# Q projected once and doubled by VectorE shuffles, h copied by VectorE, z one maximum later

## The reference

```python
h = tok(x)                                   # (16, 221, 128): three patch projections, bias, position
z = layernorm(h); q, k, v = split(z @ w_qkv.T)
a = softmax(q @ k.T / sqrt(16)) @ v          # per head
h = h + a @ w_agg.T + b_agg
z = layernorm(h)                             # first 1024 tokens, two experts each
h = h + sum_k weight_k * (gelu(z @ w1[e_k]) @ w2[e_k])
```

## Time and profile before

| | |
|---|---|
| median of 3 runs | 271.49 us (271.13 to 271.51) |
| profiled execution | 271.6 us, its span 270.0 us |
| granted TensorE clock over the span | 0.991 |
| TensorE busy | 255.9 us (95%) |
| VectorE busy | 211.9 us (78%) |
| ScalarE busy | 143.3 us (53%) |
| GpSimd busy | 114.9 us (43%) |

### The profile page before, as it was taken

How to read it: one execution, slowest core, us unless ns; L and a number is a source line. 1 busy time by engine, 2 the same in 40 slices (tenths; PEclk the granted TensorE clock), 3 DMA queues, 4 the chain that set the end, 5 groups by cost and what they waited for, 6 DMA issues and landing times.

```text
span 270.0 us, 7288 instructions
## 1 busy us (share of the span) xinstructions
PE 255.9 (95%) x2925; PEld 222.1 (82%) x2925; DVE 211.9 (78%) x453; ACT 143.3 (53%) x223; POOL 114.9 (43%) x178
## 2 busy tenths in 40 slices
PE   8999989999899999999998999999999999998991
PEld 8899977879697979797977979888888888887771
DVE  2976489879989878898968869696969697877684
ACT  4770332725251615252447676777768585869240
POOL 4000031203348474747573546656474838353200
PEclk9999999999999999999999999999999999999996
DMA  6999200089100000000021102011111111000252
GB/s 210 417 389 438 125 1 2 0 277 301 48 24 14 23 14 26 13 27 9 28 51 30 47 12 54 30 40 39 40 39 43 40 30 39 13 26 31 84 143 85
DMA packets 15623, 22.29 MB, mean 83 GB/s; under 512 B 2415, under 2 KB 10327, under 8 KB 15559
## 3 DMA queue, kind: packets, MB, share of 16 engines
q1 hardware_dynamic: 13447, 18.67, 21.1%
q0 software_dynamic: 1760, 2.60, 3.1%
q10 hardware_dynamic: 384, 0.57, 0.7%
HBM read 17.43 MB, written 5.95 MB: 87 GB/s over the span
## 4 chain that ended last, share of the span: by engine, by line
PE 70%; DVE 15%; ACT 6%; issue 4%; DMA 2%; POOL 1%; SPq 0%; DVEq 0%; POOLq 0%; ACTq 0%
PE e_ps L1153 11%; PE s_ps L1239 11%; PE s_ps L1153 8%; PE e_ps L1435 7%; PE m_ps L1353 7%; PE m_ps L1420 5%; PE m_ps L1224 5%; DVE nmax L903 4%; ACT L668 3%; PE e_ps L1420 3%; PE m_ps L1214 3%; DMA x_raw<-x 2%; PE m_ps L1383 2%; DVE x_lo L790 2%; PE m_ps L1203 1%
## 5 line engine op out<-in xcount | busy, mean ns | idle before, releaser
L903 DVE TENSOR_REDUCE nmax<-s_ps 128x4 fp32r<-128x884 f32 (+1 forms) x60 | 61.8, 1070 | 15.5 <-PE s_ps L1239 14.8
L620 ACT ACTIVATE probs<-s_ps 128x888 f32<-128x888 f32 (+1 forms) x60 | 51.4, 910 | 23.2 <-PE s_ps L1239 23.2
L517 POOL DMA_INDIRECT y_rows<-y_sb,idx_u x23 | 23.1, 1003 | 28.4 <-PE s_ps L1239 25.6
L462 POOL TENSOR_TENSOR var_eps<-mv,eps_t 128x2 f32<-128x2 f32 x16 | 5.6, 350 | 68.8 <-DVE mv L862 68.8
L495 POOL DMA_INDIRECT z_slots<-z,slot_u x20 | 23.4, 1170 | 15.8 <-PE s_ps L1239 11.4
L1353 PE MATMUL m_ps<-probs,v_aug 128*32 128x221 f32 (+1 forms) x480 | 25.8, 353 | 0.0
L1435 PE MATMUL e_ps<-w_now,hidT 128*128 128x128 f32 x184 | 23.2, 275 | 0.0
L1435 PEld LDWEIGHTS e_ps<-w_now,hidT 128*128 128x128 f32 x184 | 22.4, 192 | 0.1
L604 ACT COPY zT<-m_ps 128x221 f32<-128x221 f32 x16 | 5.5, 344 | 30.0 <-PE m_ps L1204 30.0
L1239 PE MATMUL s_ps<-k_a,q_hi 32*128 32x222 f32 (+1 forms) x252 | 19.1, 309 | 2.0 <-DVE nmax L903 1.1
L1153 PE MATMUL e_ps<-x_hi,w_hi 128*128 128x252 f32 (+2 forms) x128 | 20.7, 294 | 0.1
(11 more groups left out here) (169 smaller groups left out, 613.9 us busy)
## 6 DMA issues: line engine op xcount, KB each, us to landing
w_raw<-wt SPq DMA_DIRECT2D x6, 512.0 KB, 10.1
x_raw<-x SPq DMA_DIRECT2D x6, 512.0 KB, 10.5
w_sb<-w SPq DMA_DIRECT2D x1, 2048.0 KB, 9.9
z_slots<-z SPq DMA_DIRECT2D x1, 1518.0 KB, 13.8
zs<-z_slots SPq DMA_DIRECT2D x7, 198.0 KB, 2.6
x_raw<-x SPq DMA_DIRECT2D x4, 256.0 KB, 5.5
out<-h SPq DMA_DIRECT2D x11, 64.0 KB
c_sb<-consts SPq DMA_DIRECT2D x1, 599.5 KB, 13.2
```

What stands on the lines that cost most here:

```text
L517: g.indirect_dma_start(y_dram, bass.IndirectOffsetOnAxis(ap=idx_u[:, at:at + 1], axis=0), y_sb[:, n % 2, i, :], None).then_inc(y_out[n % 2 ...
L620: s.activation(probs[0:n, blk, 2 * f:2 * f + 2].rearrange("p t u n -> p t (u n)"), s_ps[0:n, 2 * f:2 * f + 2, 0:2 * NE], ACT.Exp, scale=DH ...
L903: v.tensor_reduce(nmax[0:n, blk, 2 * f:2 * f + 2, DH:DH + 2], src, AX_X, ALU.max, negate=True).then_inc(max_ready, 1)
```

## The change

For batches from DOUBLED = 8 on, q is projected with one weight matrix (`once`, each head's rows one time). VectorE then writes its rows twice, with two `stream_shuffle` instructions, into a new SBUF tile `q_d`; `q_high` and `q_low` read that tile. `project_v` waits for the shuffles instead of for `q_low`. In cycles 7 to 14, `q_high` stands behind `k_high` on ScalarE, `q_low` and `ln_stats` behind `k_low` on VectorE, and v is copied by ScalarE.

From cycle 7 on (batches 9 to 15) h is copied out of its bank by VectorE behind `take_max`, ahead of the shuffles, instead of by ScalarE behind the table load. For batches from LATE_Z = 9 on, `ln_z` stands in the next cycle between the two maxima, `z_turn` behind the second first-scores block, `zT_copy` behind the copy of `pv`'s result, and `keep_h` no longer waits for z. The weights' transfer grows from 320 to 384 KB.

```diff
@@ ScalarE
             def q_high(b):
-                act.wait_ge(q_done, b + 1)
-                s.copy(q_hi[:, b % 2, :, 0:N],
-                       m_ps[:, 0, 0:2 * N].rearrange("p (u n) -> p u n", u=2)).then_inc(q_hi_ready, 1)
+                if b >= DOUBLED:
+                    act.wait_ge(q_d_ready, 2 * (b - DOUBLED) + 2)
+                else:
+                    act.wait_ge(q_done, b + 1)
+                s.copy(q_hi[:, b % 2, :, 0:N], q_src(b)).then_inc(q_hi_ready, 1)
...
+                if LATE_Z <= c + 1 < BATCH:
+                    zT_copy(c + 1)
                 gelu(n, 1)
                 gelu(n, 2)
                 gelu(n, 3)
                 if experts:
                     load_table(ACT.Exp)
-                if experts and c + 2 < BATCH:
-                    h_copy(c + 2)
-                if 0 <= c + 1 < BATCH:
+                if 0 <= c + 1 < DOUBLED:
                     q_high(c + 1)
...
                 if 0 <= c + 1 < BATCH:
                     k_high(c + 1)
+                if DOUBLED <= c + 1 < BATCH:
+                    q_high(c + 1)
...
                 if 0 <= c < BATCH:
                     exps(c, 1)
+                if DOUBLED <= c + 1 < BATCH:
+                    late_v_copy(c + 1)
@@ VectorE
+TWICE = tuple([DH * u + i % DH for i in range(32)] for u in range(2))
+            def late_h_copy(b):
+                dve.wait_ge(h_turned, b + 1)
+                dve.wait_ge(hb_ready, b)
+                dve.wait_ge(z_ready, 2 * b)
+                v.tensor_copy(h_sb[:], m_ps[:, 1, 0:2 * P].rearrange("p (t d) -> p t d", t=2)).then_inc(h_ready, 1)
+            def q_double(b):
+                dve.wait_ge(q_done, b + 1)
+                for u in range(2):
+                    v.stream_shuffle(q_d[:, u, :], m_ps[:, 0, 0:N], TWICE[u]).then_inc(q_d_ready, 1)
...
+                if c + 1 >= LATE_Z and c + 1 < BATCH:
+                    ln_z(c + 1)
                 if 0 <= c < BATCH - 1:
                     maxima(c, 1)
...
                     take_max(c)
+                if 0 <= n and c + 2 < BATCH:
+                    late_h_copy(c + 2)
+                doubled = DOUBLED <= c + 1 < BATCH
+                if doubled:
+                    q_double(c + 1)
                 if c - 1 >= 0:
                     turn(c - 1)
...
-                if 0 <= c + 1 < BATCH:
+                if 0 <= c + 1 < BATCH and not doubled:
                     q_low(c + 1)
-                if c + 2 < BATCH:
+                if c + 2 < BATCH and not doubled:
                     ln_stats(c + 2)
...
                     k_unit(c + 1)
                     k_low(c + 1)
-                if c + 2 < BATCH:
+                if doubled:
+                    q_low(c + 1)
+                    if c + 2 < BATCH:
+                        ln_stats(c + 2)
+                if c + 2 < min(LATE_Z, BATCH):
                     ln_z(c + 2)
...
-                if 0 < c + 1 < BATCH - 1:
+                if 0 < c + 1 < DOUBLED:
                     v_copy(c + 1)
@@ TensorE
-                for u in range(2):
-                    mm = pe.matmul(m_ps[:, 0, u * N:(u + 1) * N], wqkv_sb[:, u, :], zT[:], start=True, stop=True)
+                if b >= DOUBLED:
+                    mm = pe.matmul(m_ps[:, 0, 0:N], wqkv_sb[:, 5, :], zT[:], start=True, stop=True)
+                else:
+                    for u in range(2):
+                        mm = pe.matmul(m_ps[:, 0, u * N:(u + 1) * N], wqkv_sb[:, u, :], zT[:], start=True, stop=True)
...
-                pe.wait_ge(q_ready, b + 1)
+                if b >= DOUBLED:
+                    pe.wait_ge(q_d_ready, 2 * (b - DOUBLED) + 2)
+                else:
+                    pe.wait_ge(q_ready, b + 1)
...
-                if ahead1:
+                if ahead1 and c + 1 < LATE_Z:
                     z_turn(c + 1)
...
                 if here:
                     s1(c, 1)
+                if ahead1 and c + 1 >= LATE_Z:
+                    z_turn(c + 1)
```

More of the change, by code:

```diff
@@ L93 @@
         3: (4, 10, 4, 10, 20), 4: (4, 10, 4, 10, 20), 5: (4, 10, 4, 10, 20), 6: (4, 10, 4, 10, 20)}
+DOUBLED = 8
+LATE_Z = 9
+TWICE = tuple([DH * u + i % DH for i in range(32)] for u in range(2))
 FIRST_ZEROS = 13
@@ L179, in build @@
         comb = sb("comb", [P, N])
-        wqkv_sb = sb("wqkv_sb", [P, 5, P])
+        wqkv_sb = sb("wqkv_sb", [P, 6, P])
         wagg_sb = sb("wagg_sb", [P, P])
@@ L275, in build @@
         g_sb = sb("g_sb", [P, FJ, TOP_K, P])
+        q_d = sb("q_d", [P, 2, N])
         nmaxT = sb("nmaxT", [P, NE], F32R)
@@ L285, in build, with q_src @@
             "p (b t u n) -> p b t u n", b=2, t=HALF, u=2)
+        def q_src(b):
+            return q_d[:] if b >= DOUBLED else m_ps[:, 0, 0:2 * N].rearrange("p (u n) -> p u n", u=2)
         def pair_of(banks):
@@ L315, in build @@
         k_hi_ready, k_ready, v_ready = sem("k_hi_ready"), sem("k_ready"), sem("v_ready")
+        q_d_ready = sem("q_d_ready")
         k_b_ready, max_in = sem("k_b_ready"), sem("max_in")
@@ L466, in keep_h @@
             def keep_h(b):
-                pool.wait_ge(z_ready, b * 2 + 2)
+                if b < LATE_Z:
+                    pool.wait_ge(z_ready, b * 2 + 2)
                 if b > 3:
@@ L633, in o_raw_copy, with late_v_copy @@
                        m_ps[:, 0, 0:2 * N].rearrange("p (r n) -> p r n", r=2)).then_inc(o_raw_ready, 1)
-            def last_v_copy(b):
+            def late_v_copy(b):
                 act.wait_ge(v_done, b + 1)
@@ L715, in _ @@
                     continue
-                if 0 <= c + 1 < BATCH:
+                if 0 <= c + 1 < LATE_Z:
                     zT_copy(c + 1)
@@ L749, in _ @@
                     exps(c, 1)
+                if DOUBLED <= c + 1 < BATCH:
+                    late_v_copy(c + 1)
                 if n == ROUNDS - 1:
-                    last_v_copy(c + 1)
                     last_y(1)
@@ L868, in ln_z @@
                                     ALU.subtract, ALU.mult).then_inc(z_ready, 1)
+            def q_double(b):
+                dve.wait_ge(q_done, b + 1)
+                for u in range(2):
+                    v.stream_shuffle(q_d[:, u, :], m_ps[:, 0, 0:N], TWICE[u]).then_inc(q_d_ready, 1)
             def q_low(b):
                 dve.wait_ge(q_hi_ready, b + 1)
-                v.tensor_tensor(q_lo[:, b % 2, :, 0:N], m_ps[:, 0, 0:2 * N].rearrange("p (u n) -> p u n", u=2),
-                                q_hi[:, b % 2, :, 0:N].bitcast(F32), ALU.subtract).then_inc(q_ready, 1)
+                v.tensor_tensor(q_lo[:, b % 2, :, 0:N], q_src(b), q_hi[:, b % 2, :, 0:N].bitcast(F32), ALU.subtract).then_inc(q_ready, 1)
             def k_unit(b):
@@ L1592 @@
     twice = np.repeat(qkv[:, 0:2].reshape(P, 2, 2, HALF, 1, DH), 2, axis=4).reshape(P, 4, P)
+    once = qkv[:, 0].reshape(P, 2, HALF, DH).transpose(0, 2, 1, 3).reshape(P, 1, P)
     arrays = {
@@ L1602 @@
                          + [a["L0_tok_scale_emb"][i] for i in range(3)], axis=1),
-        "wqkv": np.concatenate([twice, qkv[:, 2].reshape(P, 1, P)], axis=1),
+        "wqkv": np.concatenate([twice, qkv[:, 2].reshape(P, 1, P), once], axis=1),
         "wagg": a["L0_attn_w_agg"].T.reshape(2, HALF, DH, P).transpose(1, 0, 2, 3).reshape(P, P),
```

## The result

The changed kernel took 274.52 us (median of 6 runs, 274.16 to 280.27), the kernel before 271.37 (6 runs beside it, 271.12 to 271.51). The ratio is 1.0112, 95% interval 1.0100 to 1.0124: about 3.0 us slower. The forecast was 273.4, range 270.6 to 275.6. The profile has the fall in its slices with 7, 5 and 5: the granted clock is 1.00 up to 254 us, 0.67 in the next 2 us and then 0.50, the 1.2 GHz level, until some 271; before it TensorE was busy for 12.5 of the 14 us from 240 on. In the cycles read here the granted clock is 1.00, the 2.4 GHz level.

The account below looks back on a forecast made before the run. TensorE's own queue was taken to set the time. Cycle 7's 2s - 0.59, cycles 8 to 12's 5 x (2s - 0.65), cycle 13's 2s - 0.78 and cycle 14's +0.25 gave +1.8 on 271.6: 273.4 us, range 270.6 to 275.6.

Parts of the forecast that it names:

- case (1): The forecast itself: s from 0.36 to 0.52, down waits for zsT_evac in seven cycles, 272.2 to 274.5 us; chance 0.52.
- s: Cost of one 128x221 shuffle from PSUM on VectorE, start to start: taken as 0.44 us, bounds 0.30 and 0.57.
- the lower bound: Least cost of one VectorE shuffle: the copy shaped like v_copy, scaled from 256 to 221 elements, 0.30 us.
- 14s - 4.37: Summed change in us over cycles 7 to 14, two shuffles in each of seven cycles; +1.8 us at s = 0.44.
- rival (3): VectorE's shuffles overlap like plain copies, s from 0.28 to 0.35; gain and stall cancel, 271.5 us; chance 0.18.
- shuffle pair under 0.62 us makes the forecast wrong: Test on the changed profile: 0.9 us was expected from the first shuffle's start to turn's on VectorE.
- The estimate of 0.50: Alternative cost in us of a 221-element shuffle, 0.39 + 0.11 from the skill page; would make the sum +2.6, 274.2.
- The two z instructions, 0.60, fit into what is left of the 1.44 idle: On VectorE ahead of the second maxima: the later z fits into idle time, so place_max comes 0.37 us earlier.
- The hand-overs: Delays along the cycle's chain: take_max to its follower 0.59 us, zsT_evac's end to down on TensorE 0.06.
- 2s - 0.59: Change of cycle 7 in us: down starts at 148.47 + 2s, against 149.06 before.
- +0.25 forecast: End of cycle 14: q_low(15) behind k_low makes the last cycle's scores start at 249.17 instead of 248.92.
- The edits costed at nothing: k_unit, k_low and q_low on VectorE, earlier exponentials, ScalarE's copy of v, the 64 KB larger weights load: no cost.

Follow-up runs that it names:

- experiment 1: Changed kernel with zsT_evac moved ahead of the shuffles and turn, behind the copy of h: 270.91 us, ratio 0.9995 to the kernel before.
- experiment 4: Changed kernel with two more shuffles, into a tile nobody reads, ahead of the real two: 278.83 us, ratio 1.0286 to the kernel before.
- experiment 2: Changed kernel with GpSimd's copies of the second weights (fetch_w2) moved behind the second scores, after z: 272.67 us, ratio 1.0062 to the kernel before.
- experiment 5: Changed kernel without doubling: two products and no shuffle for every batch, h on VectorE and later z kept: 269.94 us, ratio 0.9956 to the kernel before.
- experiment 6: Changed kernel with h copied by ScalarE again, doubling and late z kept: 275.81 us, ratio 1.0159 to the kernel before.
- experiment 3: Changed kernel with both zsT_evac ahead of the shuffles and GpSimd's fetch_w2 copies later: 266.43 us, ratio 0.9831 to the kernel before.
- experiment 7: Changed kernel with zsT_evac ahead and fetch_w2 later, but without the doubling: 268.19 us, ratio 0.9885 to the kernel before.

## Why the prediction came out as it did

**Direction and place were right; the size came out near by luck.** "`down` waits for `zsT_evac` in seven cycles" is the first row of waits after; experiment 1 removes it by order alone and experiment 4 doubles it. The time, 274.5, lies at the upper end of case (1) (272.2 to 274.5) and 1.1 over the value; the four executions behind the ratio have a median of 274.3. But the condition of case (1), s from 0.36 to 0.52, did not hold, and two terms behind the sum were wrong in opposite ways.

**s was too large.** Taken 0.44, measured 0.305: the lower bound, the copy scaled to 221 elements, was the nearest row, and the different masks cost nothing (LOAD_MASK_SELECT 0.01). With it 14s - 4.37 is -0.1, rival (3)'s 271.5. The prediction's own test says that a "shuffle pair under 0.62 us makes the forecast wrong"; the pair is 0.61, and by the sum alone there should have been no loss. The Trainium skill, "Vector Engine (DVE) Microarchitecture Reference", section 3.8, has the selectors written by a separate instruction; the trace agrees and gives its price. The estimate of 0.50 from the Trainium skill, "VectorE: DVE Perf Modes", perf-mode tier table and section on the TRN2 errata, was farther off: it resembles the duration, 0.41, more than the spacing.

**"The two z instructions, 0.60, fit into what is left of the 1.44 idle" is the step that failed.** They took 1.42 to the next start, because the later z fell beside `fetch_w2`'s copies. `z_turn` waited 0.28 for them, and `place_max` came 6.58 after the cycle's start, not 6.26: +0.32 in each of cycles 9 to 13. The sum had looked for a late z only in the maxima, and these start just 0.08 later in the cycle than in cycle 8; the loss came through `z_turn`. Experiments 2, 5 and cycle 8 show z at 0.59 without that company, experiments 1 and 6 at 2.04 and 1.95 where it meets GpSimd otherwise. GpSimd's copies don't change with it: beside z they take 1.72 or 1.73 for three, as in the trace before, where no z runs beside them. The forecast had looked at what stands on VectorE around z, not at what GpSimd does at the place where z was moved to. The Trainium skill, "SBUF — State Buffer", section "Who interferes with whom", says that an fp32 copy or tensor_scalar of VectorE in SBUF may take a port pair that it shares with GpSimd, and that who comes second is blocked for the whole instruction. The traces agree that the two collide; that it is this port is the page's word, as no run here varies the operands. That only z pays is not what one would read out of it: in experiments 1 and 6 a z instruction starts 0.11 and 0.14 before the first copy by the traces and still takes 1.38 and 1.40, until the second copy is over.

**The hand-overs were a little short.** `take_max` to the copy of h took 0.65, not 0.59 (+0.06); `zsT_evac`'s end to `down` 0.14, not 0.06 (+0.08): the 0.06 came from `hidden`'s wait in the earlier trace rows; `down` to the next cycle 4.52, not 4.45 (+0.07). Added up for one cycle: 2 x 0.305 - 0.65 + 0.32 + 0.06 + 0.08 + 0.07 = +0.49, measured 0.48. Cycle 8, whose z is short, has the same without the 0.32: 0.17, measured 0.18.

**The ends.** Cycle 7 was forecast as 2s - 0.59, which is +0.02 at the measured s; it was 0.17, again the hand-over and the tail (0.08 + 0.07). Cycle 14: +0.25 forecast, 0.30 measured. The edits costed at nothing (k_low and q_low behind the stall, v) show no wait of their own in cycles 7 to 13, and with the larger load of weights cycle 7 starts at 137.97 against 138.01. From there to the first scores of batch 15, at full clock, TensorE's busy time is 106.1 us against 107.4: it fell, but by less than the forecast's 3.

So the errors partly cancelled: s too large by 14 x 0.135 = 1.9 us, z and the hand-overs too small by some 3.1. The slow z cost 1.4 us by experiment 2 and 1.6 by 5 x 0.32; without it 1.7 us of loss are left (experiment 2 against the kernel before). Open is whether z's 0.79 in experiment 3 comes from the indirect DMA that GpSimd issues beside it there (194.86 to 195.92, z from 195.14). In experiments 2 and 7, with 0.59, that DMA is over before z, and so it is in cycle 14 of experiment 3, again with 0.59; but no run moved it by itself. Open is also why the hand-over to `down` takes longer than that to `hidden`.

## What to carry to other kernels

A transfer between two queues that has 0.7 us of room is a wait in waiting: before work is put ahead of it, look for what on that engine nobody waits for, and place the evacuation that TensorE needs first. When an instruction is moved, read the trace at its new place on every engine, not only its own queue: here a VectorE operation that moved beside GpSimd's copies took 2.5 times as long, and up to 3.5 times in the experiments. Two covered losses hide each other; remove both before judging an edit, as the doubling looked like a loss in the changed kernel and is worth 1.5 us in experiment 3.

## What the runs showed of the hardware

- Two shuffles 128x221 from PSUM with different masks, back to back: 0.41 us each, 0.305 start to start, mask load 0.01 us. They overlap like plain copies.
- Two z instructions (tensor_scalar, 128x128 fp32, SBUF to SBUF) take 0.59 us alone and 1.50 and 1.95 beside GpSimd's copies of 128x512 fp32, and 2.04 where the first of them ran beside an indirect DMA of GpSimd. The copies beside them take 1.72 or 1.73 for three.
- A semaphore from VectorE to a `down` that had been waiting on TensorE took 0.14 us, against 0.06 to `hidden` before the change.
